# Causal mask moved into VectorE's row-minimum pass, and half of q's rotation moved to ScalarE and GpSimd

## What is computed

```python
q = einsum('btm,mhd->bthd', x, w_aq); k = ...; v = ...
q = _rope(q); k = _rope(k)      # even*cos - odd*sin, even*sin + odd*cos, halves of 64
s = einsum('bihd,bjhd->bhij', q, k) / 128
s = s - 1e30 * (i < j)
p = softmax(s, axis=-1)
o = einsum('bhij,bjhd->bihd', p, v)
r = einsum('bihd,hdm->bim', o, w_ao)
```

## Time and profile before

| | us |
|---|---|
| median of 3 runs | 1289.47 (1289.21 to 1291.32) |
| profiled execution, its own time | 1292.28 |
| its span in the trace | 1290.4 |
| PE busy | 1146.1 (89%) |
| DVE busy | 913.9 (71%) |
| POOL busy | 743.0 (58%) |
| ACT busy | 609.0 (47%) |

### The profile page before, as it was taken

One profiled execution on the slowest core, in us unless ns is written; L12 is line 12 of the kernel. 1 busy time (PEld: TensorE's weight loads), 2 busy tenths in 40 slices (PEclk: granted clock), 3 DMA queues, 4 the chain that ended last, 5 costly groups with the idle time before them and its releaser, 6 DMA issues. The chain is left out here.

```text
span 1290.4 us, 21944 instructions
## 1 busy us (share of the span) xinstructions
PE 1146.1 (89%) x7255; PEld 982.8 (76%) x7255; DVE 913.9 (71%) x1980; ACT 609.0 (47%) x1306; POOL 743.0 (58%) x783
## 2 busy tenths in 40 slices
PE   3899999999999999999999988015999999999995
PEld 2688887888878878878878863004999999999994
DVE  5788888898898898998988853775555555554422
ACT  3455555545545545545555543102554554554541
POOL 3676686676776766775766630006644844844425
PEclk9999999999999999999999999556999999999997
DMA  5000100100100100100000001304423523523212
GB/s 183 1 18 1 38 30 0 37 28 0 41 24 0 41 24 0 41 24 33 28 5 33 18 1 34 106 0 133 111 37 100 129 38 99 129 37 99 34 17 33
DMA packets 42170, 57.60 MB, mean 45 GB/s; under 512 B 8896, under 2 KB 34944, under 8 KB 41984
## 3 DMA queue, kind: packets, MB, share of 16 engines
q0 software_dynamic: 13824, 21.24, 9.1%
q1 hardware_dynamic: 28288, 35.58, 8.2%
HBM read 35.71 MB, written 16.91 MB: 41 GB/s over the span
## 5 line engine op out<-in xcount | busy, mean ns | idle before, releaser
L1125 DVE TENSOR_TENSOR hT_lo<-hid,hT_hi 128x512 fp32r<-128x512 f32 x128 | 89.2, 698 | 179.1 <-ACT hT_hi L1243 166.2
L268 ACT ACTIVATE prob<-bank,row_min 128x512 f32<-128x512 f32 (+3 forms) x256 | 135.9, 531 | 112.7 <-DVE row_min L389 112.6
L199 POOL TENSOR_SCALAR prob<-prob,row_inv 128x512 f32<-128x512 f32 (+3 forms) x256 | 134.5, 536 | 68.4 <-DVE row_inv L393 66.9
L1241 ACT ACTIVATE hid<-up,b_e 128x512 f32<-128x512 f32 x128 | 88.0, 688 | 155.0 <-PE up L1308 141.7
L339 DVE TENSOR_TENSOR pT_lo<-bank,pT_hi 128x384 fp32r<-128x384 f32 (+1 forms) x192 | 114.4, 596 | 50.2 <-ACT pT_hi L248 50.1
L949 POOL DMA_INDIRECT got<-routed_rows,tokens x64 | 86.3, 1349 | 103.4 <-DVE tokens L1119 84.9
L212 POOL TENSOR_TENSOR kT_lo<-k_cos,kT_hi 128x512 fp32r<-128x512 f32 x64 | 82.4, 1288 | 78.1 <-ACT kT_hi L248 78.1
L248 ACT ACTIVATE oT_hi<-bank 128x512 fp32r<-128x512 f32 x64 | 38.3, 599 | 185.7 <-PE bank L519 175.7
L206 POOL TENSOR_TENSOR q_cos<-q_cos,q_sin 128x512 f32<-128x512 f32 x64 | 82.3, 1286 | 55.4 <-DVE q_sin L376 55.2
L969 POOL DMA_INDIRECT out<-y,tokens x64 | 103.8, 1622 | 17.3 <-issue 14.8
L389 DVE TENSOR_REDUCE row_min<-bank 128x1 f32<-128x512 f32 (+3 forms) x256 | 112.6, 481 | 0.2
(11 more groups left out here) (196 smaller groups left out, 3853.0 us busy)
## 6 DMA issues: line engine op xcount, KB each, us to landing
raw<-in_w SPq DMA_DIRECT2D x16, 1024.0 KB
emb_res<-emb SPq DMA_DIRECT2D x8, 512.0 KB, 3.7
out<-h SPq DMA_DIRECT2D x8, 512.0 KB, 3.0
routed_rows<-x SPq DMA_DIRECT2D x8, 512.0 KB
x<-in_wq SPq DMA_DIRECT2D x1, 1024.0 KB, 6.1
x<-in_wk SPq DMA_DIRECT2D x1, 1024.0 KB, 9.6
x<-in_wv SPq DMA_DIRECT2D x1, 1024.0 KB, 4.9
x<-in_wo SPq DMA_DIRECT2D x1, 1024.0 KB, 8.5
```

What stands on the lines that cost most here:

```text
L199: nc.gpsimd.tensor_scalar(pr, pr, row_inv[:, h % 2, k:k + 1], 1.0, ALU.mult, ALU.mult).then_inc(s["norm_done"], 1)
L268: nc.scalar.activation(prob[:, h % 2, col:col + w], s_ps[bk][:, pc:pc + w], ACT.Exp, bias=row_min[:, h % 2, k:k + 1], scale=-1.0, accum_ou ...
L1125: nc.vector.tensor_tensor(out, in_, hi.bitcast(F32), ALU.subtract)\
L1241: nc.scalar.activation(hid[:, t % 2, :], up_ps[t % 2][:], ACT.Gelu, bias=bias)
```

## The change

1. The mask matmuls (`L564`) and their bfloat16 tables are gone. A row `mask_row` holds zeros and, in its last 128 columns, the scaled mask. `minimum` becomes one pass of DVE that adds `mask_row`, scales by -1/128, writes the result to `prob` in SBUF, and gives the row's minimum. `exp` then works in place on `prob`.
2. q is rotated with the same table as k. DVE keeps the cosine multiply. Two copies on ACT (`swap`) move the halves crosswise from PSUM to `q_sin`; POOL multiplies `q_sin` by the sine and then adds.
3. The score banks are handed back to PE after the minimum pass, no longer after the exponential. `v`'s first block and the next transposes wait for `q_swap` in place of `q_rope`.
4. Sequences 1 to 6 are written out instead of looped.

```diff
-            with eng.Fori(1, B - 1) as b:
+            for b in range(1, B - 1):
                 body(b, range(8), lambda h: True)
...
+            nc.gpsimd.memset(mask_row[:, 0:T - P], 0.0).then_inc(s["mask_ready"], 1)
...
             def add(b, h, x):
-                after(pool, f"{x}_rope", n + 1)
+                if x == "q":
+                    cos, sin = q_cos, q_sin
+                    after(pool, "q_swap", n + 1)
+                    nc.gpsimd.tensor_tensor(sin[:], sin[:], rope_t[:, 1, :], ALU.mult)\
+                        .then_inc(s["q_sin"], 1)
+                    after(pool, "q_sin", n + 1)
+                else:
+                    cos, sin = k_cos, k_sin
+                    after(pool, "k_rope", n + 1)
                 nc.gpsimd.tensor_tensor(cos[:], cos[:], sin[:], ALU.add).then_inc(s[f"{x}_add"], 1)
...
-                after(act, "t_done", 3 * (n - 2) + 3)
-                nc.scalar.activation(prob[:, h % 2, col:col + w], s_ps[bk][:, pc:pc + w], ACT.Exp,
+                pr = prob[:, h % 2, col:col + w]
+                nc.scalar.activation(pr, pr, ACT.Exp,
...
+            def swap(b, h):
+                n = b * H + h
+                after(act, "q_mul", n + 1)
+                after(act, "q_add", n)
+                nc.scalar.activation(q_sin[0:64, :], proj_ps[0][64:128, :], ACT.Copy)
+                nc.scalar.activation(q_sin[64:128, :], proj_ps[0][0:64, :], ACT.Copy)\
+                    .then_inc(s["q_swap"], 1)
...
+                    if live:
+                        swap(b, h)
                     if ok(h - 3):
                         after(act, "o_done", n - 3 + 1)
...
+            def rope_q(b, h):
+                n = b * H + h
+                after(dve, "q_proj", n + 1)
+                after(dve, "q_lo", n)
+                nc.vector.tensor_tensor(q_cos[:], proj_ps[0][:], rope_t[:, 0, :], ALU.mult)\
+                    .then_inc(s["q_mul"], 1)
...
-                nc.vector.tensor_reduce(row_min[:, h % 2, k:k + 1], s_ps[bk][:, pc:pc + (ib + 1) * P],
-                                        AX.X, ALU.min).then_inc(s["s_min"], 1)
+                nc.vector.tensor_tensor_reduce(prob[:, h % 2, col:col + w], s_ps[bk][:, pc:pc + w],
+                                               mask_row[:, T - w:T], scale=-1.0 / D, scalar=3e38,
+                                               op0=ALU.add, op1=ALU.min,
+                                               accum_out=row_min[:, h % 2, k:k + 1])\
+                    .then_inc(s["s_min"], 1)
...
                     if ok(h - 1):
+                        after(dve, "t_done", 3 * (n - 3) + 3)
                         after(dve, "s_done", 3 * (n - 1) + 1)
                         minimum(b, h - 1, 0)
...
-                    last = nc.tensor.matmul(s_ps[bk][:, pc + ib * P:pc + w], ident_bf[:], mask_bf[:],
-                                            start=False, stop=True)
...
-                        after(pe, "exp_done", TB * (n - 1))
+                        after(pe, "s_min", TB * (n - 1))
                         scores(b, h - 1, [0])
-                        after(pe, "exp_done", TB * (n - 2) + 3)
                         scores(b, h - 1, [1, 2])
```

More of the change, by code:

```diff
@@ L86, in build_attention @@
         o_ps, t_ps = bank[4], [bank[5], bank[4], bank[5]]
-        names = """wq_in wk_in wv_in wo_in tables_in w_hi w_lo consts
+        names = """wq_in wk_in wv_in wo_in tables_in mask_ready w_hi w_lo consts
             ids_in emb_in res_in stats_done aggr_done var_eps rstd_done xn_ready xt_tr xt_hi xt_lo
-            q_proj k_proj v_proj q_rope k_rope q_add k_add q_hi k_hi q_lo k_lo v_hi v_lo
+            q_proj k_proj v_proj q_mul q_swap q_sin k_rope q_add k_add q_hi k_hi q_lo k_lo v_hi v_lo
             s_done s_min exp_done inv_done norm_done t_done t_hi t_lo o_done o_hi o_lo
@@ L250, in _ @@
             act.wait_ge(s["tables_in"], 48)
[L251 to L254, removed]
+            nc.scalar.activation(mask_row[:, T - P:T], mask_f, ACT.Copy, scale=-float(D))\
+                .then_inc(s["mask_ready"], 1)
             def xt(b):
@@ L366, in xt, with turn_k @@
                     low_of(xT[1][:, kt, :], proj_ps[kt][:], xT[0][:, kt, :], "xt_lo")
-            def rope(b, h, x):
+            def rope_q(b, h):
                 n = b * H + h
[L370 to L377, removed]
+                after(dve, "q_proj", n + 1)
+                after(dve, "q_lo", n)
+                nc.vector.tensor_tensor(q_cos[:], proj_ps[0][:], rope_t[:, 0, :], ALU.mult)\
+                    .then_inc(s["q_mul"], 1)
+            def turn_k(b, h):
+                n = b * H + h
+                ps = proj_ps[1]
+                after(dve, "k_proj", n + 1)
+                after(dve, "k_lo", n)
+                nc.vector.tensor_tensor(k_cos[:], ps[:], rope_t[:, 0, :], ALU.mult)
+                nc.vector.tensor_tensor(k_sin[0:64, :], ps[64:128, :], rope_t[0:64, 1, :], ALU.mult)
+                nc.vector.tensor_tensor(k_sin[64:128, :], ps[0:64, :], rope_t[64:128, 1, :], ALU.mult)\
+                    .then_inc(s["k_rope"], 1)
             def t_low(b, h, f):
@@ L439, in layernorm2 @@
                     normalise2(b - 1, range(2 * half, 2 * half + 2))
-            after(dve, "w_hi", 4)
+            dve.wait_ge(s["mask_ready"], 2)
+            after(dve, "w_hi", 1)
             low_of(w_qkv["q"][1][:], wraw["q"], w_qkv["q"][0][:], "w_lo")
@@ L444, in _ @@
             aggregate(0)
-            after(dve, "w_hi", 5)
+            after(dve, "w_hi", 2)
             low_of(w_qkv["k"][1][:], wraw["k"], w_qkv["k"][0][:], "w_lo")
@@ L448, in _ @@
             xt(0)
-            after(dve, "w_hi", 6)
+            after(dve, "w_hi", 3)
             low_of(w_qkv["v"][1][:], wraw["v"], w_qkv["v"][0][:], "w_lo")
@@ L456, in body @@
                     if live:
-                        rope(b, h, "q")
+                        rope_q(b, h)
                     if ok(h - 2):
@@ L461, in body @@
                     if live:
-                        rope(b, h, "k")
+                        turn_k(b, h)
                     if isinstance(b, int) and b == 0 and h == 0:
-                        after(dve, "w_hi", 7)
+                        after(dve, "w_hi", 4)
                         low_of(w_o[1][:], wraw_o, w_o[0][:], "w_lo")
@@ L525, in xt @@
                 for kt in range(KT):
-                    after(pe, "k_rope" if kt else "q_rope", b * H)
+                    after(pe, "k_rope" if kt else "q_swap", b * H)
                     for tb in range(TB):
@@ L550, in values @@
                 g, jb = divmod(V_SLOT[h][i], TB)
-                after(pe, "k_rope" if i else "q_rope", n + 1)
+                after(pe, "k_rope" if i else "q_swap", n + 1)
                 products(proj_ps[i][:], [([t[:, kt, jb * P:(jb + 1) * P] for t in xT],
@@ L560, in scores @@
                     w = (ib + 1) * P
[L561 to L565 removed]
+                    last = products(s_ps[bk][:, pc:pc + w],
+                                    [([q[:, h % 2, ib * P:(ib + 1) * P] for q in qT],
+                                      [x[:, h % 2, 0:w] for x in kT])])
                 last.then_inc(s["s_done"], 1)
@@ L654, in body @@
                     if ok(h - 1):
-                        after(pe, "exp_done", TB * (n - 1) + 1)
+                        after(pe, "s_min", TB * (n - 1) + 1)
                         scores(b, h - 1, [3])
```

15 lines of the change are left out of this document (5 added, 10 removed).

## The result

The changed kernel takes 1347.25 us (median of 4 runs, 1346.57 to 1348.86), the kernel before 1290.39 on the same chip: a ratio of 1.0441, 95% interval 1.0424 to 1.0457. It is 4.4% slower; the span grew from 1290.4 to 1345.5, by 55.1.

A forecast was written before the change was run, and what follows sets the result against it. A ring of in-order DVE, POOL and ACT queues, 10.41 us a slot, was taken as the bound, close to PE's 10.94. Growing to 11.42, it adds 56.5 us over all sequences to 1289.5: 1346, range 1326 to 1372.

The forecast's parts named there:

- the ring: Chain through the in-order queues of DVE, POOL and ACT from one q_cos to the next: 10.41 us, forecast 11.42.
- PE is not the bound: In attention, PE at 97.5% busy doesn't set slot 4; the rival that it does, masks pure gain: 1259, 4%.
- The sum: Slot growth added over all sequences: 7.4 in each of six middle ones, 6.9 last, about 5 first; 56.5 us.
- PE's limit without masks: Removing four mask weight loads a slot takes at most 0.48 off PE's plain slot, 10.94 to about 10.46 us.
- q_cos to add, 3.24: From DVE's q_cos to POOL's add, with two ACT copies and POOL's multiply: 2.14 becomes 3.24 us, 1.10 more.
- DVE's relief, 0.29: With two DVE passes fewer, pT_lo fill 0 follows pT_hi sooner, 0.29 us less a slot.
- Minimum pass and exponential, 0.16: Minima 0 and 3 on DVE cost 0.08 more a slot; exp 0 and 1 from SBUF, 0.08 more.
- The rival of a slow pass: The new DVE minimum pass takes twice the reduce's time, 65 us more: 1411; 8% for above 1372.
- Slot by slot: Growth per sequence: slots 3, 4, 7 1.01 each; 5, 6 1.54 each; 0 0.06; 1 and 2 together 1.26 us.
- the added 0.16: In slots 5 and 6, the minimum pass and exponential items, added to the multiply's 1.38 for 1.54 us.
- Layernorm passes hit by POOL: POOL's extra work slows a quarter of DVE's eight layernorm passes a sequence by 0.9 each: 14 us, 1360.
- Signs of being wrong: Four: copies overlap off the ring, POOL passes shorten, new pass exceeds 0.75, PE's clock falls below 1.00 when idle.

The follow-up runs named there:

- the rotation alone: The kernel before with q's crosswise copies on ACT and sine multiply on POOL, masks still by matmul: 1346.91 us, ratio 1.0434.
- Masks only: The changed kernel with q rotated on DVE again by two sine multiplies, masks still added in the minimum pass: 1290.16 us, ratio 1.000.
- the two runs with ACT's order and q on DVE: Changed kernel, q rotated on DVE, pT_hi fill 0 before qT_hi, exp 1 and pT_hi fill 1 before kT_hi: 1290.86 us; with POOL's queue reordered too: 1277.08.
- the run with ACT's new order: The changed kernel with pT_hi fill 0 ahead of qT_hi, and exp 1 and pT_hi fill 1 ahead of kT_hi, on ACT: 1290.12 us, ratio 0.9999.

## Why the prediction was right, and where its terms were off

The time was 1347.25 where 1346 was said, and the chain that it gives for the changed kernel is the one that the runs show: the rotation alone brings the loss, the ring without the multiply is shorter by the multiply, and with the ring cut in ACT's queue the loss is gone. Point by point:

- *PE is not the bound.* Right for the changed kernel, where PE waits 0.79 in slot 4, and right in that the mask matmuls, taken out alone, gave 1.000. For the kernel before it goes too far. There PE has no idle time in slots 0 to 5; it waits only at the end of a sequence. The windows of slots 4 and 7, columns as in the earlier trace rows, and PE's first matmul of two q projections four slots apart:

```profile
158.55:168.96 10.41, 10.41 (x68) 8.99 (x67) 8.75 (x19) 5.59 (x15) 8.22 (x9) 1.00 0.05 15
...
194.46:205.38 10.92, 8.65 (x57) 6.98 (x56) 9.37 (x19) 6.08 (x16) 5.52 (x5) 1.00 0.00 0
```

```profile
134.36 0.47 PE L519 MATMUL bank<-xT_hi,wq_hi 128*128 128x512 f32 x1
...
178.12 0.47 PE L519 MATMUL bank<-xT_hi,wq_hi 128*128 128x512 f32 x1
```

The two are 4 x 10.94 apart, PE's own pace. The 10.41 of slot 4 is DVE catching up on it: its q_cos starts 1.67 behind the projection where it waits for PE, 2.54 behind after the evacuation, 2.31 at the start of slot 4 and 1.78 at its end. So before the change the ring had about 0.5 to spare in a plain slot, and used it up once a sequence for the evacuation. The sum isn't touched by this, since it adds up all eight distances of q_cos.
- *PE's limit without masks.* It fell less than said: slot 1 is 10.93 or 10.94 in the four kernels with mask matmuls and q rotated on DVE, and 10.54 to 10.56 in the seven without mask matmuls in which the ring is cut or short. That is 0.39 a slot, not 0.48.
- *q_cos to add, 3.24.* It is 3.33: 0.69 to the first copy, 0.61 from copy to copy (0.48 was said, the one part clearly off), 0.67 to the multiply, 1.36 to the add. A copy of 64 rows costs 0.59, as long as one of 128, so the choice of the 128-row price held. (The bound from below was reckoned wrong, without effect on the sum: 0.59 for the pair in place of 0.48 + 0.59 takes off 0.48, not 0.56.)
- *DVE's relief, 0.29.* pT_lo follows pT_hi by 0.50, 0.30 less. Told exactly, before the change DVE's own queue, not pT_hi, released pT_lo, and the way through POOL and ACT had 0.3 to spare, so the ring as listed did have some slack; the moved multiply first used that up.
- *Minimum pass and exponential, 0.16.* Masks only shows 0.09 in slot 4 (10.50 against 10.41). The pass is 0.68 like the reduce, and the whole change is no longer than the rotation alone. The rival of a slow pass is out. (The prediction's terms for its upper end come to 1375, 1361 + 14, where 1372 was said.)
- *Slot by slot.* Said 1.01 for slots 3, 4 and 7, 1.54 for 5 and 6, 0.06 for 0 and 1.26 for 1 and 2; measured 0.91, 0.92 and 0.89; 1.34 and 1.33; -0.01; 1.11. In sum 6.49, not 7.4. The ring's forecast of 11.42 is 0.09 too long: the stretch to the add cost 0.09 more than said, and the small additions came to 0.03 (0.92 - 1.19 + 0.30) instead of 0.20. POOL's norm ends at 167.02, before the copies, and costs nothing here; qT_hi starts 1.33 behind the add, 1.41 before. In slots 5 and 6 the multiply with its semaphore (1.36) is the whole growth, and the added 0.16 was wrong.
- *The sum.* Between the q_cos of slot 0 of sequences 1 and 7 the kernel lost 40.3 against 44.6 said; up to the first of these q_cos 4.8 against 5; from the q_cos of slot 0 of sequence 7 to the last evacuation 8.5 against 6.9: the last three slots, which have no head to project and for which I had put nothing, grew by about 2.4. Behind attention 1.4 more, also not in the sum. That the total came out within 1.3 us is in part the luck of a sum.
- *Layernorm passes hit by POOL.* In the changed kernel not more than before: a pass took 401/522/1298 ns in the earlier trace rows and now this (tile x, 100 to 740 us, min/median/max):

```profile
L450 DVE TENSOR_SCALAR x<-h,mean_var,rstd x24: 399/496/1341, 185.6 to 682.7; 128x256 f32<-128x256 f32 x24
```

The mechanism behind this rival is real all the same, as the two runs with ACT's order and q on DVE show (median 1249 ns against 402, 2.15 us in slot 5). It depends on which POOL instruction lies beside the pass, not on how many there are in a slot.
- *Signs of being wrong.* One of the four that the prediction named did occur, the granted clock below 1.00, in 2 of the 64 windows of 10 us between 100 and 740 us (last section). The multiply stayed at 1.29, the new pass at 0.68, and the copies are in the ring.
- *The rule of two-input passes.* The 1.12 estimated from the Trainium skill (GPSIMD Engine Reference, section 3.1) was an underestimate here; 64 multiplies took 1289 ns in the mean, as the row said.

POOL's extra pass hurt mostly by its place: the run with ACT's new order has the same passes and no loss. It still costs there in slot 6, 15.57 against 13.78 with q's sines on DVE and the same order; whether by its load or by its place in POOL's queue isn't shown.

## What to carry to other kernels

When the busiest engine stands near full, follow one period of the timeline and write down what released each instruction: the second limit may be 5% away, and whatever is added there beyond that gap costs its length, while what is taken off the busy engine may be worth nothing. Follow the busy engine's own row over several periods too: a short distance on another engine can be that engine catching up. Before moving work to an idle engine, look at what stands behind it in each in-order queue; here the head that waited for q held up two others, and the order of ACT's queue alone was worth the whole 57 us. Look for the waits inside the loaded queue too: small work put where POOL waited anyway gave 9 us. And when a reordering gains nothing, compare the lengths of the passes and not the waits alone.

## What the runs showed of the hardware that was not expected

- A layernorm pass on DVE (128x256, `tensor_scalar`, SBUF to SBUF) takes 0.40 with nothing or a gather beside it on POOL. Beside a two-input pass of POOL it can last until that pass has ended, up to 1.52: the pair at 173.79 above ends at 176.20, POOL's add at 176.04. The new minimum pass, with one input from SBUF, isn't affected: 0.68 to 0.69 in all 64 instances of 512 columns, 62 of them beside such a POOL pass.
- Two ACT copies of 64x512 from PSUM crosswise to SBUF, each 0.59, start 0.61 apart: they don't overlap as v_hi and kT_hi do (0.48 apart in the earlier trace rows). Why isn't shown; both write `q_sin`.
- `tensor_tensor_reduce` with a PSUM and a bfloat16 SBUF input and an SBUF output costs no more than a plain reduce of the bank: 0.68 for 512 columns, 0.55 for 384, 0.28 for 128, and the accumulator's read of 0.08 overlaps its end.
- PE's granted clock, 1.00 in every window of 10 us between 100 and 740 before, fell to 0.83 in two of them after, the first and the last row below. Just ahead of 510.74 PE stood idle for 1.70 (the row below them). These falls are no large part of the loss: in masks only the mean of a window was below 1.00 in four windows, with no loss of time.

```profile
490.00:500.00 10.00, 8.21 (x39) 6.51 (x39) 6.50 (x23) 5.27 (x14) 8.32 (x9) 0.83 0.05 15
500.00:510.00 10.00, 8.61 (x59) 7.66 (x57) 7.01 (x17) 4.73 (x10) 6.64 (x8) 1.00 0.00 1
510.00:520.00 10.00, 9.26 (x42) 7.92 (x43) 6.34 (x15) 5.61 (x14) 6.81 (x8) 0.83 0.00 0
```

The timeline of PE in the changed kernel, the first matmul of a sequence:

```profile
510.74 0.80 PE L545 MATMUL bank<-xT_hi,wq_hi 128*128 128x512 f32 x1 [1.70 <-DVE xT_lo L353]
```
